# Node projections moved from a stage of their own into the scatter loop of a graph kernel's first sort

## The reference, cut to what matters

```python
q = (x @ Wq.T + bq).reshape(n, H, HD)      # n = 6250, H = 8, HD = 16
k = (x @ Wk.T + bk).reshape(n, H, HD)
v = (x @ Wv.T + bv).reshape(n, H, HD)
attn = einsum('ehd,ehd->eh', q[row], k[col]) / sqrt(HD)
attn = attn + silu(edge_length @ We1.T + be1) @ We2.T + be2
cut = 0.5 * (cos(edge_length * pi / CUTOFF) + 1.0) * (edge_length < CUTOFF)
attn = attn * cut
attn = softmax of attn over the edges of each row
out = segment_sum(attn[:, :, None] * v[col], row) @ Wo.T + bo
```

## Time and profile before

| | |
|---|---|
| median of 3 runs | 9238.56 us (9234.02 to 9243.33) |
| the profiled execution | 9236.35 us, span 9234.6 us |
| busy, share of the span | POOL 67%, PE 60%, DVE 56%, ACT 25% |
| first sort, scatter loop | 152.5 to 1308.2 us |
| stages between the sort and the score pass | to 1442.3 us |

### The profile page before, as it was taken

One profiled execution on the slowest core, in us unless ns is written; L12 is line 12 of the kernel. 1 busy time (PEld: TensorE's weight loads), 2 busy tenths in 40 slices (PEclk: granted clock), 3 DMA queues, 4 the chain that ended last, 5 costly groups with the idle time before them and its releaser, 6 DMA issues. The chain is left out here.

```text
span 9234.6 us, 123780 instructions
## 1 busy us (share of the span) xinstructions
PE 5496.5 (60%) x32296; PEld 4870.9 (53%) x32296; DVE 5125.7 (56%) x14717; ACT 2272.5 (25%) x4142; POOL 6173.5 (67%) x6249
## 2 busy tenths in 40 slices
PE   6777757777729998036777755777733333333334
PEld 5666646777717776025666644666623333333333
DVE  7666654444479998045777743454554444444445
ACT  0111111111127776023444433444420000000000
POOL 2777755777717777757777717777627777577774
PEclk8555558888857777558899965555555555655556
DMA  1000006777716765015555533433311111211111
GB/s 30 2 2 2 2 23 188 210 209 210 208 37 161 166 162 129 2 55 141 137 138 135 131 33 77 78 78 78 64 32 53 52 52 53 55 52 52 52 53 47
DMA packets 877285, 793.86 MB, mean 86 GB/s; under 512 B 310468, under 2 KB 752200, under 8 KB 876542
## 3 DMA queue, kind: packets, MB, share of 16 engines
q1 hardware_dynamic: 535552, 375.25, 16.8%
q0 software_dynamic: 211680, 354.89, 15.7%
q10 hardware_dynamic: 129688, 59.67, 2.3%
HBM read 694.58 MB, written 94.60 MB: 85 GB/s over the span
## 5 line engine op out<-in xcount | busy, mean ns | idle before, releaser
L1426 PE MATMUL sum_ps_sum<-sum_hot,sum_msg 128*128 128x128 f32 x3528 | 842.0, 431 | 1413.3 <-DVE acc L1395 1361.7
L1426 PEld LDWEIGHTS sum_ps_sum<-sum_hot,sum_msg 128*128 128x128 f32 x3528 | 771.1, 330 | 1484.3 <-DVE acc L1395 1420.7
L558 POOL DMA_INDIRECT payload_dst<-place_dst_pay,place_dst_at_i x882 | 927.1, 1051 | 352.0 <-issue 303.7
L443 POOL DMA_INDIRECT payload_src<-load_src_pay_slot,load_src_at_i x882 | 862.4, 978 | 438.7 <-issue 275.8
L1370 POOL DMA_INDIRECT sum_rows<-x_table,dst_other x882 | 843.9, 957 | 457.7 <-issue 268.5
L1071 POOL DMA_INDIRECT scores_rows<-kv_table,scores_idx x882 | 834.0, 946 | 403.6 <-issue 250.5
L1494 POOL DMA_INDIRECT attend_rows<-h_table,dst_other x882 | 880.6, 998 | 306.1 <-issue 268.0
L1494 POOL DMA_INDIRECT attend_rows<-xl_table,dst_other x882 | 881.6, 1000 | 295.4 <-issue 268.5
L1370 POOL DMA_INDIRECT sum_rows<-conv_table,dst_other x882 | 843.9, 957 | 348.8 <-issue 268.5
L1566 PE MATMUL attend_ps_sum<-attend_hot,attend_msg 128*128 128x128 f32 x3528 | 677.2, 368 | 510.6 <-DVE acc L1727 510.6
L1566 PEld LDWEIGHTS attend_ps_sum<-attend_hot,attend_msg 128*128 128x128 f32 x3528 | 623.0, 273 | 555.2 <-issue 478.2
(11 more groups left out here) (441 smaller groups left out, 13655.0 us busy)
## 6 DMA issues: line engine op xcount, KB each, us to landing
attend_win<-xr_table SPq DMA_DIRECT2D x882, 68.0 KB
scores_win<-q_table ACTq DMA_DIRECT2D x882, 64.0 KB
spill<-scores_rows SPq DMA_DIRECT2D x126, 448.0 KB
place_dst_key_all<-key_rows_dst SPq DMA_DIRECT2D x126, 448.0 KB
place_dst_rows<-spill SPq DMA_DIRECT2D x126, 448.0 KB
attend_rel_all<-rel_flat_dst SPq DMA_DIRECT2D x252, 224.0 KB
place_dst_low_all<-low_rows_dst SPq DMA_DIRECT2D x126, 224.0 KB
payload_src<-load_src_pay_slot,load_src_at_i POOLq DMA_INDIRECT x882
```

What stands on the lines that cost most here:

```text
L443: pool.indirect_dma_start(o.payload, bass.IndirectOffsetOnAxis(ap=at_i[:, s, j:j + 1].bitcast(U32), axis=0), pay_slot[:, s, j, :], None).t ...
L558: pool.indirect_dma_start(o.payload, bass.IndirectOffsetOnAxis(ap=at_i[:, t:t + 1].bitcast(U32), axis=0), pay[:, t, :], None).then_inc(sca ...
L1426: mm = pe.matmul(ps_sum[:, n, j, :], msg[:, n, j, :], hot[:, n, j, :], start=True, stop=True)
```

## The change

The five stages between the sort and the score pass are dissolved:
- The turns of the five weights move to the end of the sort's counting block: PE turns them behind its sum products, ACT copies them out.
- The projections move into the first 50 of the 63 rounds of the scatter loop, one node tile in each round of two groups. ACT copies the node rows to `xs` and later the turned rows to `xt`; PE turns (`turn_nodes`) and multiplies (`node_products`); DVE adds the bias into `y` (`node_rows`); SP stores `y` one round later, between its two waits for landed scatters. `xs`, `xt`, `y` and the PSUM they use are single buffers.
- The fold runs on DVE behind its part of the scatter loop.
- The real and length copies run on DVE beside ACT's copies in `rows_to_columns`.
- The cutoff runs inside the score pass, ahead of the loops of DVE and ACT, in buffers borrowed from `acc`.

The diff, cut to what the loops do (the functions `node_tables`, `transpose_weights`, `cutoff` and the stage around the fold are deleted, and `gnn_kernel` passes the new arguments):

```diff
-def sort_edges(nc, c, o, key_d, other_d, weight_d, real_d, counts, count_next, weights, spare):
+def sort_edges(nc, c, o, key_d, other_d, weight_d, real_d, counts, count_next, weights, spare, turns, x, tables, fold):
...
+                    act.wait_ge(weights_turned, 1)
+                    for n, (dst, src) in enumerate(turns):
+                        rows_n, cols_n = src.shape
+                        act.copy(dst, ps_key[0:cols_n, n, 0:rows_n]).then_inc(copied, 1)
+                    act.wait_ge(copied, 1 + len(turns))
...
+                pe.wait_ge(weights_in, 16 * len(weights))
+                for n, (dst, src) in enumerate(turns):
+                    rows_n, cols_n = src.shape
+                    mm = pe.transpose(ps_key[0:cols_n, n, 0:rows_n], src, c.ident[0:rows_n, 0:rows_n])
+                mm.then_inc(weights_turned, 1)
...
+        table_w, table_b, stores = tables
+        xs, xt, y = st.sb("xs", [P, P]), st.sb("xt", [P, P]), st.sb("y", [P, 3 * D])
+        ps_x, ps_y = ps_sums[:, 0:P], ps_sums[:, P:P + 3 * D]
...
-                pipelined(pe, R // 2, 2, spread_keys, look_up)
+
+                def turn_nodes(i):
+                    pe.wait_ge(x_taken, i + 1)
+                    pe.wait_ge(y_ready, i + 1)
+                    pe.transpose(ps_x, xs[:], c.ident[:]).then_inc(x_turned, 1)
+
+                def node_products(i):
+                    pe.wait_ge(xt_ready, i + 1)
+                    pe.matmul(ps_y, xt[:], table_w, start=True, stop=True).then_inc(produced, 1)
+
+                def two_groups(i, more, nodes):
+                    if nodes:
+                        turn_nodes(i)
+                    spread_keys(i, 1)
+                    look_up(i, 0)
+                    if nodes:
+                        node_products(i)
+                    if more:
+                        spread_keys(i + 1, 0)
+                    look_up(i, 1)
+
+                spread_keys(0, 0)
+                with pe.Fori(0, NB) as i:
+                    two_groups(i, True, True)
+                with pe.Fori(NB, R // 2 - 1) as i:
+                    two_groups(i, True, False)
+                two_groups(R // 2 - 1, False, False)
...
+                def stage_and_snap(i, s):
+                    gi = 2 * i + s
+                    act.wait_ge(slot_free, gi + 1)
+                    act.copy(pay_slot[:, s].rearrange("p g f -> p (g f)"),
+                             group(pay[:].rearrange("p t f -> p (t f)"), gi, 4)).then_inc(staged, 1)
+                    for j in range(G):
+                        k = (s * G + j) % 2
+                        act.wait_ge(ran, gi * G + (j + 1))
+                        act.copy(running[:, k, :], ps_run[:, 0:HB]).then_inc(snapped, 1)
+
+                with act.Fori(0, NB) as i:
+                    act.copy(xs[:], x[:, bass.ds(i, 1), :].rearrange("p o d -> p (o d)")).then_inc(x_taken, 1)
+                    stage_and_snap(i, 0)
+                    act.wait_ge(x_turned, i + 1)
+                    act.copy(xt[:], ps_x).then_inc(xt_ready, 1)
+                    stage_and_snap(i, 1)
+                with act.Fori(NB, R // 2) as i:
                     for s in range(2):
-                        gi = 2 * i + s
-                        act.wait_ge(slot_free, gi + 1)
-                        act.copy(pay_slot[:, s].rearrange("p g f -> p (g f)"),
-                                 group(pay[:].rearrange("p t f -> p (t f)"), gi, 4)).then_inc(staged, 1)
-                        for j in range(G):
-                            k = (s * G + j) % 2
-                            act.wait_ge(ran, gi * G + (j + 1))
-                            act.copy(running[:, k, :], ps_run[:, 0:HB]).then_inc(snapped, 1)
+                        stage_and_snap(i, s)
...
-                pipelined(dve, R // 2, 2, compare, place)
-                if True:
-                    dve.tensor_copy(count_next[:], ps_counts[:, 0:HB]).then_inc(next_copied, 1)
-                    dve.wait_ge(next_copied, 1)
+                dve.sem_inc(y_ready, 1)
+
+                def node_rows(i):
+                    dve.wait_ge(produced, i + 1)
+                    dve.wait_ge(kept, 32 * (i + 1))
+                    dve.tensor_tensor(y[:], ps_y, table_b, ALU.add).then_inc(y_ready, 1)
+
+                def two_groups(i, more, nodes):
+                    compare(i, 1)
+                    place(i, 0)
+                    if more:
+                        compare(i + 1, 0)
+                    place(i, 1)
+                    if nodes:
+                        node_rows(i)
+
+                compare(0, 0)
+                with dve.Fori(0, NB) as i:
+                    two_groups(i, True, True)
+                with dve.Fori(NB, R // 2 - 1) as i:
+                    two_groups(i, True, False)
+                two_groups(R // 2 - 1, False, False)
+                dve.tensor_copy(count_next[:], ps_counts[:, 0:HB]).then_inc(next_copied, 1)
+                dve.wait_ge(next_copied, 1)
+                fold(Chain(dve, folded))
...
-                with sp.Fori(0, R // 2) as i:
+                sp.sem_inc(kept, 32)
+
+                def freed(i, s):
+                    sp.wait_ge(scattered[s], 16 * G * (i + 1))
+                    sp.sem_inc(slot_free, 1)
+
+                freed(0, 0)
+                freed(0, 1)
+                with sp.Fori(1, NB + 1) as i:
+                    freed(i, 0)
+                    sp.wait_ge(y_ready, i + 1)
+                    for table, c0, w in stores:
+                        sp.dma_start(table[bass.ds(i * P - P, P), :], y[:, c0:c0 + w]).then_inc(kept, 16)
+                    freed(i, 1)
+                with sp.Fori(NB + 1, R // 2) as i:
                     for s in range(2):
-                        sp.wait_ge(scattered[s], 16 * G * (i + 1))
-                        sp.sem_inc(slot_free, 1)
+                        freed(i, s)
+                sp.wait_ge(kept, 32 * (NB + 1))
...
+            [(o.real[:], rows[:, :, 3]), (o.length[:], rows[:, :, 2])])
...
+                    act.wait_ge(turn_ready, 1)
+                    act.activation(v[:], u[:], ACT.Sin, bias=half_pi[:, 0:1], scale=-two_pi).then_inc(sined, 1)
...
+                if bias_mode:
+                    link = Chain(dve, cut_steps)
+                    link(dve.memset(half_pi[:], two_pi / 4))
+                    link(dve.tensor_scalar(u[:], o.length[:], 0.5 / CUTOFF, None, ALU.mult))
+                    link(dve.tensor_copy(ui[:], u[:]))
+                    link(dve.tensor_copy(v[:], ui[:]))
+                    link(dve.tensor_tensor(u[:], u[:], v[:], ALU.subtract))
+                    link(dve.scalar_tensor_tensor(u[:], u[:], -1.0, u[:], ALU.mult, ALU.max))
+                    link(dve.tensor_scalar(v[:], u[:], -1.0, 1.0, ALU.mult, ALU.add))
+                    link(dve.tensor_tensor(u[:], u[:], v[:], ALU.min))
+                    dve.sem_inc(turn_ready, 1)
+                    link(dve.tensor_scalar(inside[:], o.length[:], CUTOFF, 0.5, ALU.is_lt, ALU.mult))
+                    dve.wait_ge(sined, 1)
+                    link(dve.scalar_tensor_tensor(cut[:], v[:], 1.0, inside[:], ALU.add, ALU.mult))
```

More of the change, by code:

```diff
@@ L331, in sort_edges @@
         hot2_ready = st.sem("hot2_ready")
+        table_w, table_b, stores = tables
+        xs, xt, y = st.sb("xs", [P, P]), st.sb("xt", [P, P]), st.sb("y", [P, 3 * D])
+        ps_x, ps_y = ps_sums[:, 0:P], ps_sums[:, P:P + 3 * D]
+        x_taken, x_turned, xt_ready, produced, y_ready, kept, folded = (
+            st.sem(n) for n in ("x_taken", "x_turned", "xt_ready", "produced", "y_ready", "kept", "folded"))
         scattered = [st.sem(f"scattered{s}") for s in range(2)]
@@ L812, in rows_by_group, with rows_to_columns @@
         rows_to_columns(nc, c, f"turn_{o.name}", [
-            (rows[:, :, 1], [o.other[:, 0:T]]), (rel[:], [o.rel[:], o.rel_bf[:]]), (rows[:, :, 2], [o.weight[:]])])
-        if o.real is not None:
-            with stage(nc, f"real_{o.name}") as st2:
-                done = st2.sem("done")
-                with nc.Block() as block:
-                    @block.vector
-                    def _(dve):
-                        dve.tensor_copy(o.real[:], rows[:, :, 3]).then_inc(done, 1)
-                        dve.tensor_copy(o.length[:], rows[:, :, 2]).then_inc(done, 1)
-                        dve.wait_ge(done, 2)
-def rows_to_columns(nc, c, name, pairs):
+            (rows[:, :, 1], [o.other[:, 0:T]]), (rel[:], [o.rel[:], o.rel_bf[:]]), (rows[:, :, 2], [o.weight[:]])],
+            [(o.real[:], rows[:, :, 3]), (o.length[:], rows[:, :, 2])])
+def rows_to_columns(nc, c, name, pairs, copies=()):
     with stage(nc, name) as st:
         ps = st.ps("turn", [P, 2, 8, P])
-        turned, copied = st.sem("turned"), st.sem("copied")
+        turned, copied, taken = st.sem("turned"), st.sem("copied"), st.sem("taken")
         with nc.Block() as block:
@@ L848, in _ @@
                 act.wait_ge(copied, sum(len(x) for _, x in pairs))
+            if copies:
```

(42 more changed lines are left out.)

149 lines of the change are left out of this document (11 added, 138 removed).

## The result

The changed kernel takes **9334.12 us** (median of 4, 9324.92 to 9337.35) against 9239.67 for the kernel before (4 runs): ratio 1.0098, 95% interval 1.0086 to 1.0111, **+94.5 us**. Forecast: 9364, +125.6, in 9270 to 9440. Of the stated cases it is the forecast one, with a pair of groups 3.9 us longer instead of 4.5.

The account below looks back on a forecast made before the run. Bound: a chain of barrier-separated stages, the scatter loop paced by GpSimd's scatters. Span 9234.6 + 216 + 2.5 + 1.7 + 1 - 95.6 = 9360.2 us, +125.6; on the median 9364 us, range 9270 to 9440.

Parts of the forecast that it names:

- the forecast one: Scatter loop: store waits make each pair of groups 4.5 us longer (3.4 to 6.4), giving 9364 us; chance 0.73.
- The mechanism and its place: Scatter loop: DVE waits for late stores across E(2i), PE's transpose waits too, delaying even groups' addresses; +4.5 us a pair.
- DVE's idle ahead of its addition: Sign in the scatter loop: an idle of 5 to 6 us before the addition, ending with the store of `kv_table`.
- the landing: Scatter loop: the two stores of 64 + 128 KB land 1.9 us after issue, bounds 1.43 and 3.8.
- GpSimd's wake-up: Scatter loop: an idle GpSimd starts its first scatter 0.9 us after the addresses are ready, against 0.3 usually.
- The slack of 1.6 us: Scatter loop before: a group's addresses are ready 1.6 us before its scatters begin.
- The removed stretch: Five stages between the last `rows_to_columns` copy and the score pass, less one barrier: 95.6 us removed.
- The weight turns: End of the counting pass: transposes and ACT copies, partly covered by DVE's last steps, cost +1.7 us, 1 to 3.
- cutoff prologue: Start of the score pass: ACT held 7.3 us, covered by 1.4 us; cost +1, or 7 if the cover fails.
- the first rival: Scatter loop: no store wait across E(2i), so nothing is late; 9146 us, chance 0.12.
- Hidden after all: Scatter loop: stores are not waited for across E(2i), so the change gains 93 us, 9146 us; chance 0.12.
- Slower by less: Scatter loop: same waits, but a pair is late by less than about 3 us, 9240 to 9305 us; chance 0.08.

Follow-up runs that it names:

- store-first kernel: Changed kernel with SP issuing the two stores ahead of its wait for the even group's landing: 9147.25 us against 9230.69 for the kernel before.
- transpose-later kernel: Changed kernel with PE's transpose of the node rows moved behind the pair's first look-ups: 9238.57 us against 9230.69 for the kernel before.
- kernel with the rest alone: Changed kernel with the projections kept in their own stage, as before: 9214.52 us against 9230.69; on the slower chips 11595.81 against 11608.72.

## Why the prediction was right, and where it was off

**The mechanism and its place were right.** `y` is a single buffer, DVE reaches `node_rows` before E(2i), and PE's transpose and DVE's comparisons stand behind it. GpSimd stalls ahead of the 48 even groups in question, each time with 3.9 to 4.3 us of idle time in its row, and no longer behind the 50th pair. At i = 49 only DVE is held:

```profile
1261.32 0.96 POOL L514 DMA_INDIRECT payload_src<-load_src_pay_slot,load_src_at_i  x1 [2.35 <-issue]
```

That is a loss of 2.05 us, where 2.5 was forecast. Besides these, seven gaps inside groups are in both kernels, at 1.7 us each before and mostly 2.2 after; together they give 3 of the 189 us, and the prediction had not seen them. DVE's idle ahead of its addition, forecast as 5 to 6 us, is 5.9 on the mean (107.0 / 18); the 7.52 of the pair shown are among the longest, since one of these gaps (at 692.64) had held GpSimd up just before.

**The pair, step by step**, in us from the end of the even group's last scatter, E = 698.97 + 0.96 = 699.93:

| step | forecast | measured |
|---|---|---|
| first store issued | 1.47 | 1.38 |
| second store issued | 2.07 | 1.91 |
| addition starts | 4.07 | 3.64 |
| look-ups begin (a PE row at 706.76) | 7.2 | 6.83 |
| addresses ready | 12.95 | 12.55 |
| first scatter | 13.85 | 13.33 |

**The mis-sized term is the landing.** It was put at 1.9 us behind the second issue, in proportion between a small and a large store, and measured 703.57 - 0.1 - 701.84 = 1.63. This and 0.16 on the issues make the 0.4 us that run through to the addresses. The rest is GpSimd's wake-up, 713.26 - 712.48 = 0.78 instead of 0.9. Together these are 0.5 to 0.6 us a pair: 48 x 3.9 + 2.05 = 189 in place of 218.5.

The Trainium skill's fixed 2.0 us plus bytes ("DMA: Bandwidth & Descriptors", "Anatomy of one DMA"), by which I had estimated 2.45, was further off than the rows. It is stated for the GpSimd path, and these stores are SyncE's; this trace has 1.63.

**The slack of 1.6 us was read too wide**, which did not enter the sum. It counts up to the start of the next scatter, but a waiting GpSimd starts only 0.78 us behind its addresses. So an estimate from these rows is that the addresses can be 1.64 - 0.78 = 0.9 us late before the loop grows.

**The smaller terms.** The removed stretch was forecast at -95.6 and measured -95.5. The row copies cost nothing: they start at 1524.35 beside ACT's copies. Nor does the fold, as the 95.5 us leave no room for it.

The weight turns do cost something, about half of the forecast 1.7 us. DVE's idle ahead of its first step in the scatter loop, kernel before and kernel after:

```profile
152.69 0.69 DVE L396 TENSOR_TENSOR load_src_one_lo<-load_src_column_g,load_src_lo_bf 128x896 bf16<-128x896 bf16 x1 [0.71 <-PEq L244]
...
153.09 0.69 DVE L446 TENSOR_TENSOR load_src_one_lo<-load_src_column_g,load_src_lo_bf 128x896 bf16<-128x896 bf16 x1 [1.62 <-PEq L246]
```

The last of ACT's copies ends at 152.12 + 0.21 = 152.33, and DVE's last step before the barrier at 151.48, so the barrier comes 0.9 us later than DVE alone would let it. That the first scatter starts at 167.6 in both kernels, from which I had concluded that the turns cost nothing, is chance: in this execution the counting had been done 0.5 us earlier, and in four other kernels with the same turns the first scatter starts at 167.9 to 168.7.

The cover of the cutoff prologue held. DVE consumes its first slot at 1561.43 + 1.08 = 1562.51, and the 22nd gather, which needs that slot, starts 1.3 us later (kernel after):

```profile
1561.43 1.08 DVE L1121 TENSOR_TENSOR scores_prod<-scores_ps_x,scores_rows 128x896 f32<-128x896 f32 x1
...
1563.82 0.95 POOL L1047 DMA_INDIRECT scores_rows<-kv_table,scores_idx  x1 [0.30 <-issue]
```

DVE's first product starts 1561.43 - 1536.84 = 24.6 us after the first gather; before it was 1459.91 - 1443.36 = 16.55. The difference is 8.0 us, forecast 7.3; the margin is 1.3, forecast 1.4; and the gather goes on with its usual 0.30.

**Two slips in the working changed nothing.** The upper end of the range by its own terms is 307 + 2.5 + 3 + 7 - 95.6 = +224, not +226. And the 1155 us given as a sign of the first rival are the window of the earlier trace rows; from first to last scatter the loop before lasts 1140.7.

**The rivals.** "Hidden after all" was priced at 9146 us on the condition that no store is waited for across E(2i). The store-first kernel fulfils the condition and took 83.4 us less than before, where the rival had -93. The rival's mechanism was right and its condition false for the changed kernel; the 10 us are the dearer issues, which no row of before had shown. "Slower by less" drew its line at 2 us a pair; the transpose-later kernel, at 2.05 to 2.1, sits on it with +7.9 us (ratio 1.0000 to 1.0018).

## What to carry to other kernels

Work that is small beside idle engines is not free when it brings a wait: look where each new wait stands in its engine's queue and what is issued behind it. When a single buffer is stored by a queue that also waits for other landings, issue the store before that wait; here this one reordering is worth 178 us (from +94.5 to -83.4). And a slack read in one trace belongs to that kind of chip: on a chip where the loop idles anyway, the same change gained 0.6%.

## What the runs showed of the hardware that was not expected

The same program took 9231 to 9240 us on some chips and 11602 to 11703 on others. The engines are busy for nearly as long on both: in the kernel with the rest alone DVE 5125.5 and 5132.5 us, GpSimd 6174.0 and 6217.4, PE 5494.3 and 5645.4 at a mean granted clock of 0.665 and 0.631. The 25% are idle time. In the scatter loop of that kernel it comes about once per round on DVE and ACT, released by "remote"; what that is, no run here showed.

On the first kind of chip, indirect scatters beside the early stores take 989 ns to issue on the mean, 978 without projections, and 977 in the changed kernel, whose stores fall beside them too. (The second kind of chip shows 990 with no projections at all, and 971 to 1007 with them.) In the store-first kernel two issues per pair are long (1.12 and 1.28 us in the pair at 642 us) where before there was one (1.18). Why the early place costs this was not separated.
